# A transformer tower with a mixture of experts: the last tile four times in its rows, and expert weights halved in four pieces instead of eight

## Chip, cores, metric

The kernel runs on one core of one Trainium2 chip. The metric is the device time of one execution in microseconds (us). The engines are TensorE (PE), VectorE (DVE), ScalarE (ACT), GpSimd (POOL) and SyncE (SP), which issues most of the transfers.

## The reference

Float32 throughout. 32 images give 36 patches and a class token each: T = 1184 tokens of 256. Cut to what matters:

```python
h = concat([class_token, patches @ W.T + b]) + pos_embedding
# attention inside a token, over its 16 heads of 16 (not over tokens)
q, k, v = heads(ln(ln(h)) @ Wq, Wk, Wv);  q = elu(q) + 1;  k = elu(k) + 1
kv  = einsum('bhnd,bhne->bnde', k, v);  qkv = einsum('bhnd,bnde->bhne', q, kv)
attn = qkv / einsum('bhnd,bnd->bhn', q, k.sum(axis=1))[..., None]
x = ln(h) + attn @ Wo + bo
x = x + gelu(ln(x) @ Wfc + bfc) @ Wproj + bproj
h = h + x
# experts choose tokens: each of 16 takes its 148 best
y = ln(h);  scores = softmax(y @ gate.T).T;  w, idx = top_k(scores, 148)
eo = (gelu(y[idx] @ Wg.T) * (y[idx] @ Wu.T)) @ Wd.T * w
out = h + scatter_add(eo, idx) + (gelu(y @ Sg.T) * (y @ Su.T)) @ Sd.T
```

## The kernel before

**Order.** The code writes out one queue for each engine by hand, with semaphores between them; an instruction waits only for its semaphores and for what stands ahead in its own queue. There are three stages: ten tiles of 128 tokens through embedding, attention and MLP; the choice of each expert's tokens; sixteen experts one after the other.

**Tiles.** `turn(t)` on every engine works on several tiles at once: the attention of tile t, the output projection of t-1 and the MLP of t-2. 1184 = 9 x 128 + 32, so tile 9 (`s9`) has 32 real rows; the other 96 are computed too, and dropped. For a tile, PE makes q, k and v (`project_qk`, `project_v`), ACT makes exp(min(q,0)) (`negate_qk`, `exp_qk`), the DVE adds max(q,0) (`combine`). Then the DVE multiplies every head of q with every head of k, as two products of 128x2048 (`qk_product`), sums over the 16 elements of a head (`qk_sum`), divides by the row's sum (`normalise`) and multiplies with v (`v_product`, again two of 2048). PE adds up the products by transposing them on top of each other (`sum_values`, 2 x 16 matmuls), ACT copies (`turn_attn`), PE projects (`project_attn`), and `copy_x1`, `squares_c`, POOL's `norm_c` (reciprocal root), ACT's `norm_c`, `turn_x2`, PE's `mlp`, ACT's `gelu`, `project_mlp` and the DVE's `add_mlp` follow. `mlp` multiplies in float16: a float32 factor is halved into a float16 and a float16 rest, and three products are added. `rest_of_x2` on POOL makes one such rest. Then come `squares_f`, `norm_f`, `turn_y` and `logits`. `early(j)` puts the first four blocks of the shared expert between the tiles.

**Choice.** After the last `logits` the DVE makes the softmax (its first step is the maximum, line 1215) and looks for each expert's threshold in ten rounds, each with one small matmul; PE fills up with the shared expert (`fill(blocks)`, `fill(downs)`).

**Experts.** Two buffers `wex_s`, one being used, one being loaded. Gate and up weights (4096 columns of float32) are halved during the expert before: ACT writes the float16 half (`split_w`, count `whi_made`), the DVE the rest (`split_w`, line 1187, count `wlo_made`). The halves lie in the tile stage's weight buffers. PE works in four pairs of hidden blocks: `gate_up(s, p)`, then ACT's `gelu_e` and the DVE's `hidden` make the pair's activations, and `down(s, p)` multiplies them with the down weights. PE's order in an expert:

```python
gate_up(s, 0); down(s.off(-1), 3); gate_up(s, 1); turn_eo(s.off(-1)); slots(s)  # slots: experts 0 to 6
down(s, 0); gate_up(s, 2); turn_x(s.off(1)); down(s, 1); gate_up(s, 3); down(s, 2)
```

`gate_up(s, 0)` waits for half of the rests of the weights, `gate_up(s, 2)` for all. A pair p of `down` with p in `in_halves(s)` is multiplied in halves too: ACT makes `halve_down` and `halve_hidden`, the DVE `rest_of_down` and `rest_of_hidden`, and PE runs 12 float16 matmuls; otherwise it runs four float32 products of two instructions each. While slots for later experts are being found (experts 0 to 6, `s.finds`; DVE's `tokens`, `hot`), only pair 0 is halved; from expert 7 on pairs 0 and 1. `copy_eoT` on ACT takes the finished sums of the expert before, `weigh` scales them, POOL gathers rows and scatters results.

Of the kernel before, what the change touches and what calls it, by code (L numbers as in the profile page):

```python
# [21 lines left out]
P = 128  # L22
# [9 lines left out]
HH = H // 2  # L32
MLP = 1024
# [39 lines left out]
def in_halves(s):  # L73

    return (0,) if s.finds else (0, 1)
# [55 lines left out]
def vit_tower(nc, patches, sel, wtok, base, wqkv, bias, wo, wfc, wproj, cols, gate,  # L131
              wsh, wsd, wex, consts, out):
    with ExitStack() as ctx:
# [151 lines left out]
        base_part = [place1(D // 2)[0:3 * BASE].bitcast(BF16) for _ in range(2)]  # L285
        wfc_raw = wex_s[0][:, 0:nfc]
        wfc16 = [as16(wfc_s)[:, b * nfc:(b + 1) * nfc] for b in range(2)]

        def w16(par, part, piece):

            if par == 0:
                return as16((wfc_s, wproj_s)[part])[:, piece * n16:(piece + 1) * n16]
            if part == 0:
                return as16(wsh_s)[:, piece * n16:(piece + 1) * n16]
            if piece < 6:
                return as16(wtok_s)[:, piece * n16:(piece + 1) * n16]
# [33 lines left out]
        w_in = {n: sem(f"in_{n}") for n in ("bias", "consts", "tok", "qkv", "o", "proj", "moe")}  # L330
# [23 lines left out]
        prod_made, num_done = sem("prod_made"), sem("num_done")  # L354
# [35 lines left out]
        def halves_by(s, i):  # L390
# [3 lines left out]
            if s.finds:  # L394
                return s.times(1, i)
# [18 lines left out]
        CHAIN_ROUNDS = 74  # L414
# [5 lines left out]
        def _(sp):  # L420
# [51 lines left out]
            sp.dma_start(wsd_s[:], wsd).then_inc(w_in["moe"], 16)  # L472
            sp.wait_ge(fclo_made, 2)
# [40 lines left out]
        def _(gp):  # L514
# [70 lines left out]
            for t in range(TILES + 1):  # L585
# [46 lines left out]
            gp.wait_ge(num_done, 2 * TILES)  # L632
# [25 lines left out]
        def _(act):  # L658
# [106 lines left out]

            def turn_x2(s):
# [1187 lines left out]
```

## Time and profile before

| what | value |
|---|---|
| median of three runs (lowest, highest) | 445.29 us (444.38, 446.16) |
| the profiled execution, its own time | 444.82 us |
| its span, first to last instruction | 442.9 us |
| busy: PE, weight loads, DVE | 415.3, 370.6, 361.4 us |
| busy: ACT, POOL | 291.7, 210.8 us |
| mean granted clock of PE | 0.987 |

The busy times are of the span. A row of a timeline joins equal neighbours (x16); in brackets stands how long the engine had been idle and what it waited for. Matmuls overlap, so the next row's start, and not the row's end, tells what a group costs.

### The profile page before, as it was taken

The numbers are of one execution on the slowest core, as the hardware profiler recorded it, in microseconds if no ns is written. First come the engines' busy times: TensorE is split into PE (matmuls) and PEld (weight loads), VectorE is DVE, ScalarE is ACT, GpSimd is POOL, SyncE is SP. The second block draws the span as 40 slices with busy tenths as digits, with TensorE's granted clock in tenths as the row PEclk, the third lists the DMA queues.
The fourth block names the chain that finished last, engine by engine and source line by source line (L and its number), as shares of the span: only waits on it lengthen the run. The fifth ranks groups of instructions, "written<-read, shape, count | busy, mean of one in ns | idle before, by whom it ended". The sixth has DMA issues, their size and how long they took to land. (4 is left out here: it accounts for less than half of the span.)

```text
span 442.9 us, 11362 instructions
## 1 busy us (share of the span) xinstructions
PE 415.3 (94%) x4188; PEld 370.6 (84%) x4188; DVE 361.4 (82%) x613; ACT 291.7 (66%) x746; POOL 210.8 (48%) x238
## 2 busy tenths in 40 slices
PE   8799999999999998997999999999999999999980
PEld 4477878988888887886787699999999999999980
DVE  3899999899999999726998588888887888888830
ACT  3564586897788766377541066777777777788840
POOL 1337637777546112332350424555555676766222
PEclk9999999999999998999999999999999999999996
DMA  8811670000000000004402399988998999997411
GB/s 287 305 60 36 236 304 1 14 13 0 13 14 11 3 13 12 3 14 157 160 1 95 80 301 313 303 292 318 301 301 275 328 326 329 335 328 226 118 17 15
DMA packets 20481, 69.31 MB, mean 157 GB/s; under 512 B 4602, under 2 KB 11236, under 8 KB 14044
## 3 DMA queue, kind: packets, MB, share of 16 engines
q1 hardware_dynamic: 14252, 60.40, 38.0%
q0 software_dynamic: 4608, 5.41, 6.1%
q10 hardware_dynamic: 1584, 3.03, 1.8%
q8 instruction: 21, 0.34, 0.3%
q14 instruction: 16, 0.13, 0.1%
HBM read 63.50 MB, written 5.33 MB: 155 GB/s over the span
## 5 line engine op out<-in xcount | busy, mean ns | idle before, releaser
L611 POOL DMA_INDIRECT xg<-token_rows,slot_g x32 | 50.2, 1569 | 72.0 <-DVE slot_g L1338 46.5
L622 POOL DMA_INDIRECT out_rows<-scratch,slot_s x32 | 53.4, 1668 | 25.2 <-ACT scratch L958 16.7
L927 ACT ACTIVATE scratch<-bank 128x296 f32<-128x296 f32 x64 | 26.5, 414 | 42.9 <-PE bank L1803 42.9
L1803 PE MATMUL bank<-scratch,wfc_s 128*128 128x148 f16 x512 | 52.5, 227 | 1.1 <-DVE scratch L1237 1.1
L1803 PE MATMUL bank<-scratch,wsh_s 128*128 128x148 f16 x512 | 52.6, 227 | 0.0
L1803 PE MATMUL bank<-scratch,wproj_s 128*128 128x148 f16 x256 | 50.6, 227 | 0.0
L1828 PE MATMUL bank<-scratch,wex_s 128*128 128x148 f32 x312 | 47.5, 295 | 0.0
L1187 DVE SCALAR_TENSOR_TENSOR wproj_s<-wex_s,wfc_s 128x512 f16<-128x512 f32 x64 | 42.1, 686 | 5.6 <-ACT wfc_s L825 4.7
L1361 DVE SCALAR_TENSOR_TENSOR scratch<-bank,scratch 128x296 f32<-128x296 f32 x64 | 29.6, 462 | 20.4 <-ACT scratch L927 20.3
L1076 DVE TENSOR_TENSOR scratch<-qk 128x2048 f32<-128x2048 f32 x20 | 45.1, 2291 | 0.7 <-PE bank L1553 0.5
L1081 DVE TENSOR_REDUCE qkt<-scratch 128x128 f32<-128x2048 f32 x20 | 44.7, 2278 | 0.0
L1803 PEld LDWEIGHTS bank<-scratch,wfc_s 128*128 128x128 f16 x512 | 42.0, 98 | 1.7 <-issue 1.2
L1803 PEld LDWEIGHTS bank<-scratch,wsh_s 128*128 128x128 f16 x512 | 42.1, 98 | 0.5
L1828 PEld LDWEIGHTS bank<-scratch,wex_s 128*128 128x128 f32 x312 | 41.2, 190 | 0.2 <-DVE scratch L1361 0.2
L1803 PE MATMUL bank<-scratch,wtok_s 128*128 128x148 f16 x192 | 39.3, 227 | 0.0
L825 ACT ACTIVATE wsh_s<-wex_s 128x512 f16<-128x512 f32 x64 | 38.0, 630 | 0.0
L825 ACT ACTIVATE wfc_s<-wex_s 128x512 f16<-128x512 f32 x64 | 37.9, 629 | 0.0
L528 POOL TENSOR_TENSOR rstd<-tmp,nhalf 128x1 f32<-128x1 f32 x38 | 35.3, 928 | 3.2
L1539 PE MATMUL bank<-wproj_s,hidT 128*128 128x256 f32 x160 | 36.4, 380 | 0.0
L1526 PEld LDWEIGHTS bank<-x,wfc_s 128*128 128x128 f16 x480 | 29.2, 101 | 8.3 <-ACT x L770 4.4
L526 POOL TENSOR_SCALAR tmp<-spread 128x1 f32<-128x1 f32 x29 | 12.1, 417 | 47.8 <-issue 31.1
L1187 DVE SCALAR_TENSOR_TENSOR wtok_s<-wex_s,wsh_s 128x512 f16<-128x512 f32 x48 | 32.3, 686 | 2.8 <-ACT wsh_s L825 2.2
(216 smaller groups left out, 1037.2 us busy)
## 6 DMA issues: line engine op xcount, KB each, us to landing
wex_s<-in_wex SPq DMA_DIRECT2D x48, 1024.0 KB, 5.1
patch_s<-in_patches SPq DMA_DIRECT2D x6, 384.0 KB, 3.1
token_rows<-y_s SPq DMA_DIRECT2D x10, 128.0 KB, 1.7
out_rows<-h_all SPq DMA_DIRECT2D x5, 256.0 KB, 6.2
wex_s<-in_wfc ACTq DMA_DIRECT2D x2, 512.0 KB, 9.7
wproj_s<-in_wproj SPq DMA_DIRECT2D x1, 1024.0 KB, 7.9
wex_s<-in_wsh SPq DMA_DIRECT2D x1, 1024.0 KB, 6.6
wqkv_s<-in_wqkv ACTq DMA_DIRECT2D x1, 768.0 KB, 8.0
```

The costliest lines, as they stand in the source:

```text
L528: return gp.tensor_tensor(rstd[:, k:k + 1], tmp[:, k:k + 1], nhalf[:], ALU.pow)
L611: gp.indirect_dma_start(xg[s.par][:, k, :], None, rows, bass.IndirectOffsetOnAxis(slot_g[s.par][:, k:k + 1], 0))\
L622: gp.indirect_dma_start(out, bass.IndirectOffsetOnAxis(slot_s[s.par][:, k:k + 1], 0), eo[2 * s.par + k], None, compute_op=ALU.add).then_in ...
L825: act.activation(w16(s.par, 0, PIECES[n]), wex_s[s.par][:, n * n16:(n + 1) * n16], ACT.Copy, scale=SPLIT).then_inc(whi_made, 1)
L1076: ve.tensor_tensor(dst.rearrange("p (h j d) -> p h j d", h=HH, j=H), q, k, ALU.mult).then_inc(v_chain, 1)
L1081: ve.tensor_reduce(qkt[:, g * HH:(g + 1) * HH, :], src.rearrange("p (h j d) -> p h j d", h=HH, j=H), AX, ALU.add).then_inc(v_chain, 1)
L1187: ve.scalar_tensor_tensor(w16(s.par, 1, PIECES[n]), wex_s[s.par][:, n * n16:(n + 1) * n16], SPLIT, w16(s.par, 0, PIECES[n]), ALU.mult, ALU ...
L1361: ve.scalar_tensor_tensor(hexT[:, 2 * p:2 * p + 2, :].rearrange("p m c -> p (m c)"), ps_up[p % 2][:, 0:2 * C], (HSPLIT if p in in_halves(s ...
L1526: last = pe.matmul(ps_fc[m // 4][:, (m % 4) * P:(m % 4 + 1) * P], wfc16[a][:, k * MLP + m * P:k * MLP + (m + 1) * P], x2_16[b][:, k, :], s ...
L1539: last = pe.matmul(ps_proj[:, 0:D], hidT[:, m, :], wproj_s[:, m, :], start=False, stop=(m == MC - 1))
L1803: last = pe.matmul(dst[p % 2][:, x * C:(x + 1) * C], w16(s.par, a, piece)[:, lo:lo + P], x16[s.par][b][:, k, :], start=(n == 0), stop=(n = ...
L1828: last = pe.matmul(ps_down[k][:, 0:C], wex_s[s.par][:, lo:lo + P], hexT[:, m, :], start=(m == 0), stop=(m == MC - 1))
```

## The change

It has two parts.

**The last tile.** The host lays the 32 rows of tile 9 four times below each other. Attention of the group of heads 4r to 4r+3 is then computed in rows 32r to 32r+31 only: the DVE's products are 128x1024 instead of four times 128x2048. The transposes on PE are 8 instead of 32, and `project_attn_last` multiplies four groups of 32 columns with four blocks of the output weights (`wo9`, four new loads on SP's queue ahead of expert 0's weights) into the first 32 rows. The queues of PE, ACT, POOL and the DVE are written in a new order around tile 9.

**The experts.** Weights are halved in four pieces of 1024 columns, not eight of 512, in a new order among the other steps; and pairs 0 and 1 are halved in all sixteen experts. The places of the halves change so that two pieces lie side by side (`two_of`).

```diff
 def in_halves(s):
-    return (0,) if s.finds else (0, 1)
+    return (0, 1)
...
+            for x in range(2):
+                for b in range(2):
+                    sp.dma_start(wo9[b * HG * HD:(b + 1) * HG * HD, x::2, :], wo[x * HG * HD:(x + 1) * HG * HD, :, :]).then_inc(w_in["o9"], 16)
             sp.wait_ge(fclo_made, 2)
             load_gu(Step(0, 0), 0)
...
 # POOL, tile loop
+                if t == TILES:
+                    norm_c(s.off(-1), after(2))
                 if t >= 2:
                     rest_of_x2(s.off(-2))
...
-                if t >= 1:
+                if 1 <= t < TILES:
                     norm_c(s.off(-1), after(2))
...
 # ACT, split_w (the DVE's in the same way)
-                    act.activation(w16(s.par, 0, PIECES[n]), wex_s[s.par][:, n * n16:(n + 1) * n16],
-                                   ACT.Copy, scale=SPLIT).then_inc(whi_made, 1)
+                    act.activation(two_of(s.par, 0, n), wex_s[s.par][:, 2 * n * n16:2 * (n + 1) * n16],
+                                   ACT.Copy, scale=SPLIT).then_inc(whi_made, 2)
...
 # ACT, end of the tiles
-            for t in range(3, TILES):
+            for t in range(3, TILES - 1):
                 turn(t)
             s9 = Step(0, TILES - 1)
+            turn_attn(s9.off(-1))
+            norm_c(s9.off(-2))
+            squares_f(s9.off(-3))
+            copy_x1(s9.off(-1))
+            turn_x2(s9.off(-2))
+            squares_c(s9.off(-1))
+            load_gelu()
+            turn_attn_last()
             norm_c(s9.off(-1))
-            turn_x2(s9.off(-1))
-            squares_f(s9.off(-2))
-            turn_attn(s9)
+            gelu(s9.off(-2))
+            norm_f(s9.off(-3))
             copy_x1(s9)
             squares_c(s9)
-            gelu(s9.off(-1), (0,))
+            turn_x2(s9.off(-1))
+            turn_y(s9.off(-3))
+            squares_f(s9.off(-2))
             norm_c(s9)
-            gelu(s9.off(-1), (1,))
+            gelu(s9.off(-1))
             turn_x2(s9)
...
-            split_w(Step(0, 0), range(0, 3))
+            split_w(Step(0, 0), (0,))
             squares_f(s9)
...
-            split_w(Step(0, 0), range(3, 6))
+            split_w(Step(0, 0), (1, 2))
             turn_y(s9)
...
 # ACT, expert
                 halve_down(s, 0)
                 if not first:
                     copy_eoT(s.off(-1))
+                halve_hidden(s, 0)
                 split(0)
-                halve_hidden(s, 0)
-                split(1)
                 gelu_e(s, 1)
-                split(2)
                 halve_down(s, 1)
                 halve_hidden(s, 1)
-                split(3)
+                split(1)
                 if not first:
                     weigh(s.off(-1))
-                split(4)
                 gelu_e(s, 2)
                 if not last:
                     turn_x(s.off(1))
-                split(5, 6, 7)
+                split(2, 3)
                 gelu_e(s, 3)
...
 # DVE, last tile: combine_last(s), then turn_last(s)
+                for r in range(GROUPS):
+                    mine, own = slice(r * LAST, (r + 1) * LAST), slice(r * n, (r + 1) * n)
+                    ve.scalar_tensor_tensor(qk[s.par][mine, 0:n], ps_qk[mine, own], 0.0, expo[mine, own], ALU.max, ALU.add)\
+                      .then_inc(own_made, 1)
+                ve.wait_ge(own_made, GROUPS)
+                ve.scalar_tensor_tensor(qk[s.par][:, D:2 * D], ps_qk[:, D:2 * D], 0.0, expo[:, D:2 * D], ALU.max, ALU.add).then_inc(qk_made, 1)
...
+                add_mlp(s.off(-3))
+                # product 128x1024, sum over 16, sum over a head's row, reciprocal, weights, product 128x1024
...
 # DVE, end of the tiles
+            halve_shared()
+            cast_marks()
             add_mlp(s9.off(-2))
-            halve_shared()
             halve_y(0, 3)
-            cast_marks()
             add_mlp(s9.off(-1))
...
 # DVE, expert
+                rest_of_hidden(s, 0)
                 split(0)
-                rest_of_hidden(s, 0)
-                split(1)
                 hidden(s, 1)
                 if not first:
                     place(s.off(-1))
-                split(2)
                 rest_of_down(s, 1)
                 rest_of_hidden(s, 1)
...
-                split(3, 4)
+                split(1)
                 hidden(s, 2)
                 if nxt:
                     split_x(s.off(1))
-                split(5, 6, 7)
+                split(2, 3)
                 hidden(s, 3)
...
 # PE, end of the tiles
-            for t in range(4, TILES):
+            for t in range(4, TILES - 1):
                 turn(t)
-            early(0, 1)
             s9 = Step(0, TILES - 1)
+            sum_values(s9.off(-1))
+            project_attn(s9.off(-1))
+            turn_x2(s9.off(-2))
+            sum_values_last(s9)
+            mlp(s9.off(-2))
+            project_attn_last(s9)
             turn_x2(s9.off(-1))
-            sum_values(s9)
-            project_attn(s9)
+            logits(TILES - 5)
+            project_mlp(s9.off(-2))
+            pe.wait_ge(x1_made, TILES)
+            turn_y(s9.off(-3))
+            early(0)
             mlp(s9.off(-1))
-            logits(TILES - 4)
             turn_x2(s9)
             project_mlp(s9.off(-1))
             turn_y(s9.off(-2))
             mlp(s9)
+            early(1)
             project_mlp(s9)
             early(2)
+            pe.wait_ge(yT_made, TILES - 3)
+            logits(TILES - 4)
```

## Rows read from the trace of the kernel before

**Rows 1.** TensorE's timeline, last tile: start, us, engine, line, operation, idle before.

```profile
167.48 0.40 PE L1526 MATMUL bank<-x,wfc_s 128*128 128x128 f16 x4 [1.50 <-ACT x L770]
168.23 4.26 PE L1526 MATMUL bank<-x,wfc_s 128*128 128x128 f16 x44 [0.35 <-POOL x L562]
...
181.26 1.97 PE L1553 MATMUL bank<-kst,scratch 128*128 128x128 f32 x16 [0.90 <-ACT x2T L741]
...
186.42 2.84 PE L1526 MATMUL bank<-x,wfc_s 128*128 128x128 f16 x48
...
190.23 0.44 PE L1440 MATMUL bank<-kst,x 128*128 128x128 f32 x2 [0.56 <-ACT x L717]
...
197.08 3.68 PE L1539 MATMUL bank<-wproj_s,hidT 128*128 128x256 f32 x16
```

**Rows 2.** VectorE's timeline, last tile and the softmax's first step.

```profile
161.62 0.68 DVE L1106 SCALAR_TENSOR_TENSOR qk<-bank,expo 128x512 f32<-128x512 f32 x1
...
174.95 2.29 DVE L1095 TENSOR_TENSOR late<-qkt,vx 128x2048 f32<-128x2048 f32 x1
...
207.56 0.32 DVE L1215 TENSOR_REDUCE mx<-bank 128x10 f32<-128x160 f32 x1
```

**Rows 3.** ScalarE's timeline in experts with search and without.

```profile
277.58 0.48 ACT L933 ACTIVATE scratch<-bank 128x148 f32<-128x148 f32 x2
...
289.11 0.48 ACT L933 ACTIVATE scratch<-bank 128x148 f32<-128x148 f32 x2
...
345.91 0.48 ACT L933 ACTIVATE scratch<-bank 128x148 f32<-128x148 f32 x2
346.27 0.63 ACT L825 ACTIVATE wsh_s<-wex_s 128x512 f16<-128x512 f32 x1
346.79 0.45 ACT L949 ACTIVATE scratch<-scratch 128x296 f16<-128x296 f32 x1
...
350.01 0.82 ACT L958 ACTIVATE scratch<-bank,weight 74x256 f32<-74x256 f32 x2
...
351.84 1.67 ACT L825 ACTIVATE wsh_s<-wex_s 128x512 f16<-128x512 f32 x3
...
356.61 0.48 ACT L933 ACTIVATE scratch<-bank 128x148 f32<-128x148 f32 x2
```

**Rows 4.** VectorE's timeline in an expert without search.

```profile
351.49 0.69 DVE L1187 SCALAR_TENSOR_TENSOR wtok_s<-wex_s,wsh_s 128x512 f16<-128x512 f32 x1 [0.15 <-ACT wsh_s L825]
...
354.65 0.46 DVE L1361 SCALAR_TENSOR_TENSOR scratch<-bank,scratch 128x296 f32<-128x296 f32 x1
```

**Rows 5.** TensorE's timeline in experts with search and without.

```profile
271.12 1.22 PE L1828 MATMUL bank<-scratch,wex_s 128*128 128x148 f32 x8
272.18 0.29 PE L1803 MATMUL bank<-scratch,wsh_s 128*128 128x148 f16 x2
...
350.01 0.42 PE L1780 MATMUL bank<-kst,xg 74*128 74x74 f32 x4
350.42 0.95 PE L1821 MATMUL bank<-scratch,x_all 128*128 128x148 f16 x12
351.21 0.29 PE L1803 MATMUL bank<-scratch,wfc_s 128*128 128x148 f16 x2
...
355.35 0.84 PE L1828 MATMUL bank<-scratch,wex_s 128*128 128x148 f32 x5
```

**Rows 6.** One line's instructions: line 1059, duration in ns minimum/median/maximum.

```profile
L1059 DVE SCALAR_TENSOR_TENSOR wfc_s<-wex_s,wfc_s x2: 1224/1225/1226, 16.2 to 18.0; 128x1024 f16<-128x1024 f32 x2
```

**Rows 7.** Stretches: busy of five engines (x instructions), granted clock, DMA share, GB/s.

```profile
168.00:170.00 2.00, 1.77 (x17) 1.77 (x18) 2.00 (x2) 1.73 (x4) 1.75 (x5) 0.57 0.00 0
204.00:208.00 4.00, 2.70 (x26) 2.27 (x24) 2.56 (x6) 3.84 (x7) 0.88 (x2) 1.00 0.48 152
```

**Rows 8.** ScalarE's timeline at the end of the last tile.

```profile
204.14 0.60 ACT L717 ACTIVATE y_s<-h_all,shift,rstd 128x256 f32<-128x256 f32 x1 [1.03 <-POOL shift L533]
204.65 1.66 ACT L825 ACTIVATE wfc_s<-wex_s 128x512 f16<-128x512 f32 x3
```

More of the change, by code:

```diff
@@ L32 @@
 HH = H // 2
+GROUPS = 4
+HG = H // GROUPS
+LAST = 32
 MLP = 1024
@@ L285, in vit_tower @@
         base_part = [place1(D // 2)[0:3 * BASE].bitcast(BF16) for _ in range(2)]
+        wo9 = place1(GROUPS * D).rearrange("p (r n) -> p r n", r=GROUPS)
         wfc_raw = wex_s[0][:, 0:nfc]
@@ L1175, in turn, with turn_last @@
                 v_product(s, 1, late[:], scaled)
-                if t + 1 < TILES:
+                if t + 2 < TILES:
                     combine(s.off(1))
-            for t in range(TILES):
+                else:
+                    combine_last(s.off(1))
+            def turn_last(s):
+                by = [P, HG, H, HD]
+                mine = prod[s.par][:, 0:HG * H * HD]
+                weights = qkt[:, 0:HG, :]
+                add_mlp(s.off(-3))
+                ve.wait_ge(qk_made, TILES)
+                q = qk[s.par][:, 0:HG * HD].rearrange("p (h d) -> p h d", d=HD).unsqueeze(2).to_broadcast(by)
+                k = qk[s.par][:, D:2 * D].rearrange("p (j d) -> p j d", d=HD).unsqueeze(1).to_broadcast(by)
+                at = after(5)
+                ve.tensor_tensor(mine.rearrange("p (h j d) -> p h j d", h=HG, j=H), q, k, ALU.mult).then_inc(v_chain, 1)
+                ve.wait_ge(v_chain, at(1))
+                ve.tensor_reduce(weights, mine.rearrange("p (h j d) -> p h j d", h=HG, j=H), AX, ALU.add).then_inc(v_chain, 1)
+                ve.wait_ge(v_chain, at(2))
+                ve.tensor_reduce(den[:, 0:HG], weights, AX, ALU.add).then_inc(v_chain, 1)
+                ve.wait_ge(v_chain, at(3))
+                ve.reciprocal(rden[:, 0:HG], den[:, 0:HG]).then_inc(v_chain, 1)
+                ve.wait_ge(v_chain, at(4))
+                ve.tensor_tensor(weights, weights, rden[:, 0:HG].unsqueeze(2).to_broadcast([P, HG, H]), ALU.mult).then_inc(v_chain, 1)
+                ve.wait_ge(v_made, TILES)
+                ve.wait_ge(v_chain, at(5))
+                a = weights.rearrange("p h j -> p j h").unsqueeze(3).to_broadcast([P, H, HG, HD])
+                v = vx[s.par][:].unsqueeze(2).to_broadcast([P, H, HG, HD])
+                ve.tensor_tensor(mine.rearrange("p (j h e) -> p j h e", j=H, h=HG), a, v, ALU.mult).then_inc(prod_made, 1)
@@ L1199, in _ @@
             add_mlp(s9)
[L1200 removed]
+            split_w(Step(0, 0), (0,))
             shared_hidden(2)
[L1202 removed]
+            split_w(Step(0, 0), (1, 2))
             shared_hidden(3)
@@ L1555, in sum_values, with sum_values_last, project_attn_last @@
                     last.then_inc(num_done, 1)
+            def sum_values_last(s):
+                pe.wait_ge(x2T_made, TILES - 2)
+                pe.wait_ge(prod_made, s.times(2, 1))
+                for n in range(H // 2):
+                    last = pe.matmul(ps_at[:, 0:P], prod[s.par][:, n * P:(n + 1) * P], ident,
+                                     is_transpose=True, start=(n == 0), stop=(n == H // 2 - 1))
+                last.then_inc(num_done, 1)
+            def project_attn_last(s):
+                pe.wait_ge(x1_made, s.n)
+                pe.matmul(ps_o[:, 0:D], ident, x_all[:, s.n, :], start=True, stop=False)
+                pe.wait_ge(attnT_made, TILES)
+                pe.wait_ge(w_in["o9"], 64)
+                for r in range(GROUPS):
+                    pe.matmul(ps_o[0:LAST, 0:D], attnT[:, 0, r * LAST:(r + 1) * LAST], wo9[:, r, :], start=False, stop=False)
+                pe.matmul(ps_o[:, 0:D], ones_b[0:BP, :], bias_s[:, B_O:B_O + D], start=False, stop=True).then_inc(o_done, 1)
             def shared_gate_up(j):
@@ L1888, in _lay_out @@
     tok[:T].reshape(IMAGES, SEQ, PATCH_K)[:, 1:] = x
+    assert T == (TILES - 1) * P + LAST
+    tok[T:] = np.tile(tok[T - LAST:T], (GROUPS - 1, 1))
     a = {"patches": np.ascontiguousarray(tok.reshape(TILES, P, TKC, P).transpose(0, 3, 2, 1))}
@@ L1894, in _lay_out @@
     sel[np.where(t % SEQ == 0, SEQ + 1, SEQ), t] = 1
+    sel[:, T:] = np.tile(sel[:, T - LAST:T], (1, GROUPS - 1))
     in_halves = np.isin(np.arange(TP) // P, SPLIT_TILES)
```

49 lines of the change are left out of this document (29 added, 20 removed).

## The prediction

> **What bounds the kernel now.** I read the table of stretches first, then TensorE's timeline, then those of VectorE (DVE) and ScalarE (ACT) at the same moments. The page says PE 94% busy, DVE 82%, ACT 66%, and the chain that ended last holds only the last scatter, so neither tells what an edit is worth. Three stages matter. In the tile loop (to 160 us) PE and DVE are both full. In the last tile (160 to 207 us) they take turns: PE has nothing ready from 165.98 us, waits twice, for ACT and for POOL, and then runs slowly [rows 1]; the DVE works on the last tile's attention until 177.24 us [rows 2]. From 253 us on the sixteen experts run, PE without a gap: one expert with pair search takes 11.53 us (289.11 less 277.58), one without 10.70 us (356.61 less 345.91) [rows 3]. What the reader is to see there is how little room is behind the full PE: the last hidden pair of an expert is ready at 354.65 + 0.46 = 355.11 us, and PE starts the matmuls that need it at 355.35 us [rows 4, 5]. With about 0.08 us for the signal the slack is 0.16 us in a round of 10.70.
>
> **The last tile on the DVE.** From the halving instruction at 512 columns, 0.69 us [rows 4], and the same at 1024, 1.225 us [rows 6], one column costs 1.045 ns and an instruction 0.15 us; the products of 2048 columns fit (2.29) [rows 2]. Removed are four products and two sums of 2048 with their small ones. In their place: combine as four pieces of 32x64 (0.21 each) and one of 256 (0.42), with overlap 1.1 us instead of 0.6; add_mlp 0.35; product 1.22, sum 1.22, three small instructions 0.75 with waits, product 1.22. From 161.62 us the last product is ready at 167.6 instead of 177.24 us.
>
> **The last tile on PE.** PE is free at 165.98 in both. Before, it waits until 168.23 us and its 48 matmuls end at about 172.3. Now `sum_values_last` stands ahead of `mlp(7)` and waits for the DVE until 167.7; eight transposes take 0.9 us at full clock (16 take 1.97) [rows 1]. The granted clock after the old gap was 0.57 in 168 to 170 us, while 1.3 us without work in 204 to 208 us left it at 1.00 [rows 7]. The new gap of 1.7 us lies between. I take it that the clock falls as before to the lower of its two levels, which makes `mlp(7)` end at 172.6, 0.3 us later than before; if it does not, at 171.4.
>
> The Trainium skill ("TensorE: Matmul & The Clock Gate", Terms and Part 1) says that the clock has just these two states and that the activity window is free-running, so that the same gap may or may not cost a fall. By that rule the new gap could go either way from run to run, and the sum would be 1.1 us better with no fall; the trace agrees as far as a gap of 1.3 us did not cost it and 1.85 us did.
>
> From there to the end of `project_mlp(9)` (197.08 + 3.68 = 200.76 us before) PE loses: 32 transposes, 3.55; the waits of 0.90 and 0.56 us before 181.26 and 190.23 [rows 1], for both of which the new order has other work (`early(0)`, `project_mlp`); the logits moved behind, 0.57 (from 189.10, where the 48 matmuls of 186.42 stop issuing, to the wait's start at 189.67); tails that these waits exposed, 0.2. It gains two more products of 256 columns in `project_attn_last`, 0.43 each as in the 3.68 us for eight, 0.85. Sum 5.0 less. The end of `project_mlp(9)` comes at about 196.0, 4.7 us earlier. The reordered queues of ACT and POOL I followed step by step: `norm_c(8)` waits for POOL ahead of `gelu(7)` until about 171.2 and costs nothing, since `project_mlp(7)` now starts at 176; the rest of `x2T` of the last tile is ready near 187.0, `mlp(9)` wants it near 187.8: that cover is thin, and each us it is late is one us of PE. The four loads of `wo9` go on SP's queue at 50 us, 0.43 us each, before weights that are needed 150 us later: nothing.
>
> **Up to the search.** What follows `project_mlp(9)` is serial: add, squares, POOL's root, `norm_f(9)` on ACT 3.38 us later (204.14 before), then halvings, and the DVE's first step of the softmax at 207.56, 3.42 us after `norm_f(9)` [rows 2, 8]. Before, three halvings of 512 stand there (first one through ACT at 204.65 + 0.63, then 3 x 0.60 on the DVE, then 0.34 for the last shared product). Now two of 1024, a third more columns: ACT starts 0.51 after `norm_f(9)`, 1.05, 0.15 for the signal, 2 x 1.14 (1.225 less the overlap of 0.08), 0.34: 4.33. So 0.9 us is given back, and the search begins 3.9 us earlier (5.0 with no fall of the clock). The search itself, 45 us, keeps its instructions: its one piece of 1024 for two of 512 lies before a wait of the DVE for PE. Front: -3.9 us.
>
> **The experts: PE.** In experts 0 to 6 the second down pair turns from 8 float32 matmuls (1.06 us from start to next start) to 12 float16 (0.79, of which the others' show a wait of 0.16 us for the halved weights before them: 350.01 + 0.25 to 350.42) [rows 5]. Alone that is 7 x 0.27 = 1.9 us less, and the pieces' new order takes the 0.16 us away in eight more, 1.3 us.
>
> **The experts: the loop behind PE.** Larger pieces save overlap only: on ACT 0.63 for 512 against, by the slope of the rows of 512 and 296 columns (0.63, 0.45), 1.05 for 1024; started back to back 1.04 (two) against 0.94. DVE 1.21 against 1.14. That is 0.4 and 0.3 us per expert; but each piece now stands whole in a loop through three engines. From the end of the last hidden pair: signal to PE 0.08; down pair 1.06; to ACT 0.20 (355.35 + 1.06 to 356.61); `copy_eoT` 0.36; `halve_hidden` 0.34; first piece on ACT 1.05; to the DVE 0.15; first piece there 1.14; `hidden(1)` 0.46; 0.03; `halve_hidden(1)` 0.34; second piece on ACT 0.94; `weigh`, `gelu_e(2)` and `turn_x` 1.31 (350.01 to 351.84 less one piece of 0.52); third piece 1.05; to the DVE 0.15; third and fourth piece there 2.28; `hidden(3)` 0.46 [rows 3 to 6]. Sum 11.40 us. The same loop before is 10.5, since the DVE works on a piece of 512 while ACT makes the next and `hidden(1)` waits behind 0.6, not 1.14 us. PE's own round is 10.54, so the eight last experts go from 10.70 to 11.40 us: 8 x 0.70 = 5.6 us more, PE waiting 0.8 us for `hidden(3)` in each. Where the search for slots makes PE's own round 11.28, the loop decides by little: 11.40 against 11.53, 5 x 0.13 = 0.65 less. The first expert with its neighbour come out even. Experts: +4.9 us. Bounds: pieces on ACT of 1.00 to 1.11 and on the DVE of 1.20 to 1.25 make it +2.2 to +7.5. What DMA brings is not late: gate and up weights are asked for about a round and a half before use, and a longer round helps them.
>
> **Sum.** -3.9 + 4.9 = +1.0 us. The profiled execution took 444.82 us (442.9 of span, 1.9 around it), which becomes 445.8; the median of the runs shown is 0.47 above the profiled one, so 446.3 us. 0.5% (2.2 us) is what a measurement can tell from nothing: no change that can be told.
>
> **Rivals.**
> - The loop is hidden after all (PE's full rounds speak for it; the slack of 0.16 us against it): the experts take PE's own time, -1.9 - 1.3, with -3.9 in front 438.2 us. It needs pieces 0.12 us cheaper than estimated at all six places. Chance 0.12.
> - The loop is longer: pieces at the upper bound, 11.6 us, now above the old round even with search: +7.8, and -3 in front, 450 us. It decides once the loop passes 11.5. Chance 0.15.
> - The last tile's gain does not arrive: `mlp(9)` waits for ACT's and POOL's `x2T`, or `gelu(7)` behind `norm_c(8)` holds `project_mlp(7)`; worth 3 us if ACT is that late: -1 + 4.9, 449.2 us. For it speaks how much ACT has in order there; against it the slack of 0.8 us and more that I found. 0.10.
> - The clock stays up after the gap at 166 us: 445.2 us. 0.20.
> - PE waits so often in the experts that its clock falls in each: at the lower clock 44 of the 48 matmuls took 4.26 us, all 48 took 2.84 [rows 1], so about 1.1 us for each fall, 8 x 1.1 more, 455 us. The Trainium skill (the same page, "HAM oscillation — how this bites in real kernels") describes loops that fall each round, with longer waits; gaps here of 0.9 and 1.3 us left the clock at 1.00 [rows 1, 7]. 0.03.
>
> **How the numbers follow.** The forecast has 0.40, with its own range 444.5 to 448. Faster by over 0.5% (below 443.1): the hidden loop and a little of the fourth rival, 0.15. Slower (above 447.5): second, third and last rival, 0.28. Same: 0.57. The range 442 to 449.5 leaves out the hidden loop, the upper part of the longer one and the falling clock, 0.20.
>
> **What would show it.** In the new trace: the last product of the last tile ends near 167.6 us; the first reduction of the softmax near 203.7; `copy_eoT` comes every 11.4 us in all experts but the first, and PE waits 0.7 to 0.8 us for `hidden(3)` before each last down pair of experts 7 to 14. If PE shows no gap there, the loop's sum is wrong; if the search starts later than 205, the order in the last tile.

## The result, and the profile after

| | before | changed |
|---|---|---|
| median on record (lowest, highest; executions) | 445.1 us (444.38, 446.16; 4) | 449.93 us (448.04, 450.74; 4) |
| ratio, 95% interval | | 1.0104 (1.0077 to 1.0131) |
| profiled execution: own time, span | 444.82, 442.9 us | 448.04, 445.6 us |
| first `combine` on the DVE, from the span's start | 20.58 us | 21.16 us |
| from there to the softmax's first step | 186.98 us | 183.31 us |
| from there to the first `copy_eoT` | 58.50 us | 58.77 us |
| the fourteen rounds from one `copy_eoT` to the next | 6 x 11.525, 8 x 10.70 us | 14 x 11.455 us |
| from the first `combine` to the last `copy_eoT` | 409.13 us | 411.37 us |

The prediction was 446.3 us with "no change that can be told"; on record the kernel became 1.0% slower, and 449.93 lies 0.4 us above the range. The lower part of the table comes from the two traces and has no start and no end in it. There the change costs 2.24 us; the forecast sum was 1.0. The profiled execution of the changed kernel was the fastest of its four, 1.89 us below their median.

The profile page after, the parts on busy time and on the costliest groups (busy us, mean ns, idle us and what ended it):

```profile
PE 414.0 (93%) x4196; PEld 366.9 (82%) x4196; DVE 355.8 (80%) x564; ACT 290.3 (65%) x696; POOL 196.2 (44%) x238
...
L1252 DVE SCALAR_TENSOR_TENSOR wproj_s<-wex_s,wfc_s 128x1024 f16<-128x1024 f32 x32 | 38.5, 1224 | 11.6 <-ACT wfc_s L845 11.6
L1921 PE MATMUL bank<-scratch,wex_s 128*128 128x148 f32 x256 | 40.2, 301 | 4.7 <-DVE scratch L1426 4.7
```

Every engine has less to do than before, and the kernel is slower: PE now waits 4.7 us in all for `hidden` ahead of a down pair. TensorE's timeline in the last tile:

```profile
168.45 1.81 PE L1626 MATMUL bank<-kst,scratch 128*128 128x128 f32 x8 [2.03 <-DVE scratch L1241]
170.05 3.79 PE L1589 MATMUL bank<-x,wfc_s 128*128 128x128 f16 x48
173.67 0.65 PE L1633 MATMUL bank<-x_all,kst 128*128 128x256 f32 x2
...
193.59 3.62 PE L1602 MATMUL bank<-wproj_s,hidT 128*128 128x256 f32 x16
```

The waits of 0.90 and 0.56 us in [rows 1] are gone, and `project_mlp(9)` starts 172.43 us after the first `combine` (193.59 - 21.16) instead of 176.50 (197.08 - 20.58). The long idle time ahead of the last tile's sums is 2.03 us, and behind it the clock is low, as in the first row of [rows 7] (the granted clock is the first number behind the five pairs):

```profile
168.00:172.00 4.00, 3.55 (x27) 3.52 (x28) 3.97 (x3) 2.36 (x5) 3.92 (x3) 0.58 0.00 0
```

The end of that stretch, on ScalarE and on VectorE, against [rows 8] and the last of [rows 2]:

```profile
200.17 0.60 ACT L733 ACTIVATE y_s<-h_all,shift,rstd 128x256 f32<-128x256 f32 x1 [0.17 <-POOL shift L547]
200.68 1.99 ACT L845 ACTIVATE wfc_s<-wex_s 128x1024 f16<-128x1024 f32 x2
```

```profile
201.86 2.36 DVE L1252 SCALAR_TENSOR_TENSOR wproj_s<-wex_s,wfc_s 128x1024 f16<-128x1024 f32 x2 [2.42 <-ACT wfc_s L845]
204.14 0.42 DVE L1151 SCALAR_TENSOR_TENSOR hsh_s<-bank,gel_sh 128x256 f32<-128x256 f32 x1
204.47 0.31 DVE L1280 TENSOR_REDUCE mx<-bank 128x10 f32<-128x160 f32 x1
```

The DVE idles 2.42 us for two pieces on ACT and then works alone: two engines in turn. From `norm_f(9)` to the softmax it is 4.30 us (forecast 4.33).

One round of a late expert: ScalarE, VectorE and TensorE, the counterparts of [rows 3 to 5]:

```profile
354.89 0.48 ACT L962 ACTIVATE scratch<-bank 128x148 f32<-128x148 f32 x2 [0.92 <-PE bank L1921]
355.25 0.45 ACT L978 ACTIVATE scratch<-scratch 128x296 f16<-128x296 f32 x1
355.59 1.06 ACT L845 ACTIVATE wfc_s<-wex_s 128x1024 f16<-128x1024 f32 x1
...
358.43 0.45 ACT L978 ACTIVATE scratch<-scratch 128x296 f16<-128x296 f32 x1 [0.95 <-DVE scratch L1426]
358.79 1.04 ACT L845 ACTIVATE wfc_s<-wex_s 128x1024 f16<-128x1024 f32 x1
359.73 0.81 ACT L987 ACTIVATE scratch<-bank,weight 74x256 f32<-74x256 f32 x2
...
361.04 2.00 ACT L845 ACTIVATE wfc_s<-wex_s 128x1024 f16<-128x1024 f32 x2
...
366.34 0.48 ACT L962 ACTIVATE scratch<-bank 128x148 f32<-128x148 f32 x2 [0.92 <-PE bank L1921]
```

```profile
356.79 1.23 DVE L1252 SCALAR_TENSOR_TENSOR wproj_s<-wex_s,wfc_s 128x1024 f16<-128x1024 f32 x1 [0.59 <-ACT wfc_s L845]
357.94 0.46 DVE L1426 SCALAR_TENSOR_TENSOR scratch<-bank,scratch 128x296 f32<-128x296 f32 x1
...
362.24 2.36 DVE L1252 SCALAR_TENSOR_TENSOR wproj_s<-wex_s,wfc_s 128x1024 f16<-128x1024 f32 x2 [0.29 <-ACT wfc_s L845]
364.51 0.89 DVE L1426 SCALAR_TENSOR_TENSOR scratch<-bank,scratch 128x296 f32<-128x296 f32 x2
```

```profile
353.57 1.27 PE L1921 MATMUL bank<-scratch,wex_s 128*128 128x148 f32 x8 [0.58 <-DVE scratch L1426]
365.03 1.27 PE L1921 MATMUL bank<-scratch,wex_s 128*128 128x148 f32 x8 [0.58 <-DVE scratch L1426]
```

Read the loop by start times. PE 353.57, ACT's copy 354.89, `halve_hidden` 355.25, first piece 355.59, the DVE's 356.79, `hidden(1)` 357.94, `halve_hidden(1)` 358.43, second piece 358.79, `weigh` 359.73, third piece 361.04, the DVE's last two 362.24, `hidden(3)` 364.51, PE again 365.03. It closes in 11.46 us and nothing in it has slack. PE shows 0.58 us of emptiness (forecast 0.7 to 0.8), and the round costs 0.755 more than before.

### The profile page after: what moved, and what is told of

The parts are those of the page before. It is cut to its first block and busy times, and to the rows that moved or that the text cites. A ratio compares the mean times of both kernels' runs of the same rounds, so it can differ in the third digit from the quotient of the medians.

```text
span 445.6 us, 11224 instructions
## 1 busy us (share of the span) xinstructions
PE 414.0 (93%) x4196; PEld 366.9 (82%) x4196; DVE 355.8 (80%) x564; ACT 290.3 (65%) x696; POOL 196.2 (44%) x238
## 5 line engine op out<-in xcount | busy, mean ns | idle before, releaser
L627 POOL DMA_INDIRECT xg<-token_rows,slot_g x32 | 36.7, 1148 | 65.3 <-DVE slot_g L1403 39.1
L1252 DVE SCALAR_TENSOR_TENSOR wproj_s<-wex_s,wfc_s 128x1024 f16<-128x1024 f32 x32 | 38.5, 1224 | 11.6 <-ACT wfc_s L845 11.6
L1921 PE MATMUL bank<-scratch,wex_s 128*128 128x148 f32 x256 | 40.2, 301 | 4.7 <-DVE scratch L1426 4.7
L1102 DVE TENSOR_TENSOR scratch<-qk 128x2048 f32<-128x2048 f32 x18 | 40.6, 2290 | 0.5 <-PE bank L1616 0.4
L1921 PEld LDWEIGHTS bank<-scratch,wex_s 128*128 128x128 f32 x256 | 33.7, 190 | 8.1 <-DVE scratch L1426 7.4
L1107 DVE TENSOR_REDUCE qkt<-scratch 128x128 f32<-128x2048 f32 x18 | 40.2, 2276 | 0.0
L1602 PEld LDWEIGHTS bank<-wproj_s,hidT 128*128 128x128 f32 x160 | 29.6, 190 | 3.8
L845 ACT ACTIVATE wsh_s<-wex_s 128x1024 f16<-128x1024 f32 x32 | 32.8, 1052 | 0.0
L845 ACT ACTIVATE wfc_s<-wex_s 128x1024 f16<-128x1024 f32 x32 | 32.8, 1051 | 0.0
L1589 PE MATMUL bank<-x,wfc_s 128*128 128x128 f16 x480 | 30.6, 223 | 0.6
```

The costliest lines, as they stand in the source:

```text
L627: gp.indirect_dma_start(xg[s.par][:, k, :], None, rows, bass.IndirectOffsetOnAxis(slot_g[s.par][:, k:k + 1], 0))\
L845: act.activation(two_of(s.par, 0, n), wex_s[s.par][:, 2 * n * n16:2 * (n + 1) * n16], ACT.Copy, scale=SPLIT).then_inc(whi_made, 2)
L1102: ve.tensor_tensor(dst.rearrange("p (h j d) -> p h j d", h=HH, j=H), q, k, ALU.mult).then_inc(v_chain, 1)
L1107: ve.tensor_reduce(qkt[:, g * HH:(g + 1) * HH, :], src.rearrange("p (h j d) -> p h j d", h=HH, j=H), AX, ALU.add).then_inc(v_chain, 1)
L1252: ve.scalar_tensor_tensor(two_of(s.par, 1, n), wex_s[s.par][:, 2 * n * n16:2 * (n + 1) * n16], SPLIT, two_of(s.par, 0, n), ALU.mult, ALU.s ...
L1589: last = pe.matmul(ps_fc[m // 4][:, (m % 4) * P:(m % 4 + 1) * P], wfc16[a][:, k * MLP + m * P:k * MLP + (m + 1) * P], x2_16[b][:, k, :], s ...
```

## The experiments

One row for each, in the order they are told. Medians in us with lowest, highest and number of executions; "before" is the kernel before, run on the same chip beside it; the last three columns are times of the trace after the first `combine` (itself in the column ahead of them). Four chips: the first four rows belong to one, the next four to a second, the next two to a third and the last two to a fourth.

| edit | median | before | ratio (95%) | first `combine` | softmax | first to last `copy_eoT` | last `copy_eoT` |
|---|---|---|---|---|---|---|---|
| changed kernel again | 447.77 (446.64, 449.32; 7) | 445.37 | 1.0065 (1.0037 to 1.0093) | 20.16 | 183.27 | 169.25 | 411.27 |
| last tile only | 442.25 (439.65, 442.99; 8) | 445.37 | 0.9927 (0.9899 to 0.9956) | 20.65 | 182.79 | 163.63 | 404.89 |
| experts only | 451.82 (449.85, 453.82; 6) | 445.37 | 1.0150 (1.0112 to 1.0189) | 23.55 | 185.60 | 169.32 | 413.68 |
| last tile, two pairs, eight pieces | 441.87 (439.73, 443.79; 10) | 445.37 | 0.9928 (0.9903 to 0.9954) | 21.12 | 182.74 | 163.46 | 405.26 |
| `hidden(3)` ahead of the last piece | 442.27 (440.96, 445.13; 6) | 445.5 | 0.9929 (0.9901 to 0.9957) | 22.81 | 183.19 | 162.37 | 404.33 |
| gap filled | 448.82 (448.12, 448.89; 4) | 445.5 | 1.0067 (1.0046 to 1.0087) | 22.04 | 183.13 | 169.26 | 411.15 |
| large pieces, old pairs | 448.0 (447.2, 450.65; 6) | 445.5 | 1.0050 (1.0032 to 1.0068) | 23.31 | 182.98 | 169.69 | 412.27 |
| gap filled and `hidden(3)` ahead | 441.75 (440.02, 442.9; 6) | 445.5 | 0.9903 (0.9880 to 0.9927) | 22.63 | 183.12 | 162.25 | 404.14 |
| gap filled, halvings held back | 447.59 (445.13, 448.2; 12) | 446.64 | 1.0009 (0.9989 to 1.0030) | 20.57 | 181.67 | 169.35 | 409.79 |
| all three | 440.54 (439.79, 441.57; 6) | 446.64 | 0.9860 (0.9832 to 0.9888) | 22.29 | 181.70 | 162.60 | 403.07 |
| before again | 449.09 (447.2, 450.02; 12) | 448.31 | 1.0012 (0.9991 to 1.0032) | 21.33 | 186.92 | 166.99 | 412.38 |
| changed, a third time | 449.0 (448.07, 450.36; 12) | 448.31 | 1.0013 (0.9992 to 1.0033) | 22.16 | 183.20 | 169.31 | 411.84 |

(For the two traces above the column "first to last `copy_eoT`" is 163.65 before and 169.29 after. From the first `combine` to that of the last tile it is 140.75 to 141.05 us in all fourteen.)

### The changed kernel again

No edit.

> The changed kernel once more. Its trace is 2.7 us longer than that of before, while the medians stand 4.8 us apart. Theory (the loop through ScalarE and VectorE, 11.46 us in every expert, minus some 3 us in the last tile): median 448 to 450, rounds of 11.46 us again. Rival (the other 2 us are the clock, which falls once more in some executions, around the new gap of TensorE at 166 us): the traces differ by the stretches of lower clock, with a mean clock of 0.982 in the longer ones.

The trace repeats itself within 0.1 us (411.27), the time does not: 0.65% above before where the record has 1.04%, and its median, 447.77 us, is just below the 448 to 450 expected. The rival on the clock is taken up where the prediction is answered.

### The last tile's part alone

The changed kernel, with the pieces, their order and the pairs of before:

```diff
-    return (0, 1)
+    return (0,) if s.finds else (0, 1)
...
-                split(2, 3)
+                split(5, 6, 7)
                 gelu_e(s, 3)
```

> Only the last tile's part; the experts as before. Theory: rounds of 11.53 and 10.70 us again, the search begins 3 to 4 us earlier, 3 us faster than before, 442. Rival (the gap at 166 us costs clock, or the new order costs elsewhere): 444 to 446, no gain.

The last tile's part is worth 4.2 us of the trace (409.13 - 404.89), and the time is 0.73% less. 0.5 us of it comes with small pieces: the softmax is at 182.79, with large ones at 183.31.

### The experts' part alone

The kernel before, with the other half of the change:

```diff
-    return (0,) if s.finds else (0, 1)
+    return (0, 1)
...
-                split(5, 6, 7)
+                split(2, 3)
                 gelu_e(s, 3)
```

> Only the experts' part (pieces of 1024, two halved pairs everywhere); the last tile as before. Theory: rounds of 11.46 us in all experts, 5.6 us slower than before plus some 0.3 from the early pieces, 451. Rival (TensorE's own work decides, pieces do not matter): 1.9 to 3 us faster, 442.

Rounds of 11.46 us: +5.7 us from first to last `copy_eoT` (169.32 against 163.65), the time 1.5% more. The softmax comes 1.4 us earlier than before with the old last tile, since here the clock stayed up behind the same gap that [rows 1] show. TensorE's timeline:

```profile
170.23 0.40 PE L1526 MATMUL bank<-x,wfc_s 128*128 128x128 f16 x4 [1.50 <-ACT x L775]
170.98 2.63 PE L1526 MATMUL bank<-x,wfc_s 128*128 128x128 f16 x44 [0.35 <-POOL x L567]
```

Before, the same 44 matmuls behind the same two waits took 4.26 us.

### The last tile with two pairs everywhere, eight small pieces

```diff
 # the last tile's part alone, and
-    return (0,) if s.finds else (0, 1)
+    return (0, 1)
```

> The last tile's part and two halved pairs everywhere, but eight pieces of 512 in the old order. Theory (the size of the pieces is the cause): rounds of about 11.4 us with search and 10.70 without, -3 in the last tile and -0.3 to -0.7 in the experts, 441.5. Rival (two halved pairs in the experts with search load ScalarE and VectorE too much): those rounds at 11.6 or more, 443 to 446.

The pairs are worth nothing that can be told: 163.46 us for the rounds against 163.63, and 0.6 us lost between the softmax and the first `copy_eoT` (59.06 us against 58.47); 0.9928 against 0.9927. The whole loss is in the pieces and their order.

### hidden(3) ahead of the last piece

```diff
 # ACT, and on the DVE hidden(s, 3) for gelu_e
-                split(2, 3)
-                gelu_e(s, 3)
+                split(2)
+                gelu_e(s, 3)
+                split(3)
```

> The changed kernel with the last of the four pieces behind gelu_e(3) on ScalarE and behind hidden(3) on VectorE; all sizes as changed. Theory: this takes 1.14 us (VectorE's piece) out of the loop of 11.46, to about 10.3, below TensorE's own work, so rounds of 11.28 with search and 10.6 without; 6 x 0.25 and 8 x 0.10 below before, with the last tile 5 to 6 us faster than before, 440. Rival (the two engines are simply slower with large pieces, or another wait of the same length takes over): rounds of 11 us or more without search, 445 or more.

Same pieces, same instructions, one of them two places later. VectorE's timeline:

```profile
351.97 0.46 DVE L1427 SCALAR_TENSOR_TENSOR scratch<-bank,scratch 128x296 f32<-128x296 f32 x1
352.35 1.22 DVE L1253 SCALAR_TENSOR_TENSOR wqkv_s<-wex_s,wsh_s 128x1024 f16<-128x1024 f32 x1
353.52 0.47 DVE L1427 SCALAR_TENSOR_TENSOR scratch<-bank,scratch 128x296 f32<-128x296 f32 x1
354.58 0.69 DVE L1450 SCALAR_TENSOR_TENSOR x_all<-wex_s,x_all 128x512 f16<-128x512 f32 x1 [0.60 <-ACT x_all L971]
```

`hidden(3)` stands behind one piece (352.35 to 353.52), and PE no longer waits for it at all: rounds of 10.65 us (one 10.87), below the old 10.70, and of 11.29 to 11.43 with search. 6.9 us less than the changed kernel in the rounds. The sizes are the same, so the loss came from where the last piece stands in the loop, not from large pieces as such. The time, 442.27 us, is 3.2 us below before on its chip and not the 5 to 6 expected: the loop was put at 10.3 us and the rounds at 11.28 and 10.6, and they are a little longer.

### The gap filled

```diff
             turn_x2(s9.off(-2))
+            for _ in range(26):
+                pe.matmul(bank[0][:, 384:512], ones_b[:], ones_b[:], start=True, stop=True)
             sum_values_last(s9)
```

Work is added here whose result nobody uses.

> The changed kernel with 26 matmuls of 128x128 float16-sized data into an unused part of a bank in the gap ahead of sum_values_last (some 1.6 of its 2.0 us). Theory: the clock then stays at its upper level and the transposes and mlp(7) take 0.9 and 2.8 us, 1.1 to 1.9 us less than in the changed kernel, 446.5. Rival (the clock falls for another reason, or the end of mlp(7) is not what the rest waits for): the search begins at the same distance from the first combine, 183.3 us.

The clock is 1.00 over 168 to 172 us, the eight transposes start every 0.11 us (0.90 in all, against 1.60) and `mlp(7)` takes 2.84. From the start of the transposes to the end of `mlp(7)` that is 3.58 us instead of 5.22 (173.67 - 168.45), 1.64 less. The softmax comes only 0.2 us earlier. What took the rest: TensorE's, then GpSimd's timeline.

```profile
169.28 1.06 PE L1627 MATMUL bank<-kst,scratch 128*128 128x128 f32 x8 [0.58 <-DVE scratch L1242]
170.18 2.84 PE L1590 MATMUL bank<-x,wfc_s 128*128 128x128 f16 x48
...
176.49 0.44 PE L1504 MATMUL bank<-kst,x 128*128 128x128 f32 x2 [0.92 <-ACT x L734]
```

```profile
169.63 1.70 POOL L582 TENSOR_TENSOR hx<-h_all,x_all 128x256 f32<-128x256 f32 x1
171.42 2.12 POOL L541 TENSOR_SCALAR tmp<-spread 128x1 f32<-128x1 f32 x1
```

PE reaches `turn_x2(8)` earlier and waits 0.92 us for ACT's `norm_c(8)`, which waits for GpSimd, whose smallest instruction takes 2.12 us there.

### Large pieces, old pairs

```diff
-    return (0, 1)
+    return (0,) if s.finds else (0, 1)
```

> The changed kernel with pair 1 of down plain again in the experts with search; pieces of 1024. Theory: TensorE's own work is the bound there, 11.53 us, and the loop of 11.46 elsewhere: 6 x 0.07 us slower than the changed kernel, 448.3. Rival (the second halved pair loads the engines): faster than the changed kernel by 1 us or more.

Rounds with search 11.525, without 11.455: PE's own round decides in the first, the loop in the second. Here the clock stayed at 1.00 behind an unfilled gap of 2.04 us, and again PE waited 0.91 us for `norm_c(8)`.

### Gap filled and hidden(3) ahead

The two diffs above in one kernel.

> f_hidden_first and g_gap_filled together. Theory: the gains add, 438.5 to 439. Rival: as f_hidden_first, since the filled gap gives nothing.

The gains did not add (438.5 to 439 us was expected): both edits together give what the second gives alone, within 0.2 us of the trace.

### The halvings held back

```diff
 # with the gap filled; DVE
-            halve_shared()
             cast_marks()
+            ve.wait_ge(c_rstd, TILES - 1)
+            halve_shared()
             add_mlp(s9.off(-2))
```

> The changed kernel with the gap before the last tile's sums filled by 26 matmuls, and with VectorE's two halvings of 2048 columns held back until GpSimd has finished norm_c(8). Theory (GpSimd's small instructions are slowed by VectorE's long halvings, 2.12 us for a 128x1 tensor_scalar, 1.70 for hx, and this holds back norm_c(8), gelu(7) and project_mlp(7), which is where the clock's gain went in the run with the gap filled): GpSimd's rows read 0.73 and 0.19 us again, ScalarE's norm_c(8) comes about 3.5 us sooner, PE's wait of 0.92 us before turn_x2 is gone, and the search begins 182.0 us after the first combine, against 183.13 with the gap filled alone; time about 1.1 us below that run's. Rival (GpSimd is late for another reason, or project_mlp(7) is held by something else): 183.1, no change. Second rival (the halvings now hold back early(0) or the next halvings): search no earlier, or later.

GpSimd's timeline, then VectorE's and TensorE's:

```profile
168.21 0.72 POOL L582 TENSOR_TENSOR hx<-h_all,x_all 128x256 f32<-128x256 f32 x1
169.02 0.19 POOL L541 TENSOR_SCALAR tmp<-spread 128x1 f32<-128x1 f32 x1
169.29 0.55 POOL L543 TENSOR_TENSOR rstd<-tmp,nhalf 128x1 f32<-128x1 f32 x1
```

```profile
171.32 1.23 DVE L1157 TENSOR_SCALAR wsh_s<-wex_s 128x2048 f16<-128x2048 f32 x1 [2.17 <-POOL shift L548]
172.59 2.29 DVE L1159 SCALAR_TENSOR_TENSOR wsh_s<-wex_s,wsh_s 128x2048 f16<-128x2048 f32 x1
```

```profile
173.99 0.38 PE L1505 MATMUL bank<-kst,x 128*128 128x128 f32 x2
174.22 0.52 PE L1671 MATMUL bank<-gate_s,yT 128*128 128x16 f32 x4
```

The instruction of 2.12 us takes 0.19, PE has no wait ahead of `turn_x2(8)`, and the softmax comes at 181.67 us, 1.46 us earlier than with the gap filled alone (1.1 expected).

### All three

This wait, the filled gap and `hidden(3)` ahead of the last piece.

> The same with the last two pieces of weights parted, hidden(3) between them (both edits that helped or might help, together). Theory: search 182.0 to 182.3 us after the first combine, experts as in the run with hidden(3) ahead of the last piece (rounds of 11.3 to 11.4 and 10.65), the last copy_eoT 403.1 us after the first combine against 404.14 with the gap filled and hidden(3) ahead; time 440.7 us. Rival (the halvings' place doesn't matter): 404.1 and 441.8 us.

403.07 us to the last `copy_eoT`, as expected (403.1), 6.1 us below before; the time is 440.54 us, 1.4% below it. This version beats both kernels.

### Before again, and the changed kernel a third time

> The kernel before, unchanged, for a second trace of it and more executions. Theory (the first 20 us vary from execution to execution whatever the change, and what the change adds is the 2.2 us between the first combine and the last copy_eoT that the traces show): the last copy_eoT comes 409.1 us after the first combine again, within 0.1 us, while the first combine itself may come anywhere from 20.2 to 23.6 us. Rival (the kernel before starts reliably early, and the changed one late, so that part of the recorded difference of 4.8 us lies in the start): first combine at 20.6 us again.

> The changed kernel, unchanged, a third time. Theory: the last copy_eoT 411.3 us after the first combine, and a time 2.2 to 2.7 us (0.5% to 0.6%) above the kernel before on the same chip. Rival (the recorded 1.0% is the change's own): 4.5 us above it.

Of the two theories only the varying start held, and neither rival did: the last `copy_eoT` came at 412.38 us for 409.1 expected and at 411.84 for 411.3. On this chip the two kernels are level: 449.09 and 449.0 us. Ten of the twelve executions of the changed kernel are within 0.9 us of its median, and its trace reads 411.84. The kernel before is slower here (448.31 and 449.09 us) than on the other chips (445.1 to 446.64), and its trace shows 3.3 us in the experts with search, rounds of 13.60, 12.06, 11.53, 11.70, 11.69 and 11.92 us. TensorE's timeline in the first, and the stretches around it:

```profile
272.04 0.29 PE L1803 MATMUL bank<-scratch,wsh_s 128*128 128x148 f16 x2 [0.34 <-issue]
...
272.82 0.40 PE L1780 MATMUL bank<-kst,xg 74*128 74x74 f32 x3 [0.43 <-issue]
273.57 0.27 PE L1780 MATMUL bank<-kst,xg 74*128 74x74 f32 x1 [0.35 <-issue]
```

```profile
270.00:271.00 1.00, 1.00 (x19) 1.00 (x17) 0.58 (x1) 1.00 (x3) 0.56 (x1) 1.00 0.96 406
271.00:272.00 1.00, 0.66 (x8) 0.37 (x6) 0.44 (x3) 0.15 (x1) 0.84 (x1) 1.00 0.61 175
272.00:273.00 1.00, 0.53 (x6) 0.34 (x5) 1.00 (x2) 0.00 (x0) 0.70 (x2) 1.00 0.05 16
273.00:274.00 1.00, 0.65 (x7) 0.52 (x7) 0.18 (x1) 0.00 (x0) 1.00 (x1) 1.00 1.30 166
```

PE stops between matmuls that wait for no engine ("issue"), and ACT runs nothing from 272 to 274 us (fourth pair of columns): no semaphore that the trace shows explains it. The third trace of the changed kernel has one such stop, of 1.27 us, ahead of its first `copy_eoT`, and so has that of the large pieces with the old pairs. What makes them, and whether they favour one kernel, stays open.

The start, too, varied: 21.33 us here against 20.58 for the same kernel, though PE began tile 0's q and k earlier. TensorE's timeline here, then in the first trace of the kernel before:

```profile
16.75 3.25 PE L1492 MATMUL bank<-wqkv_s,xnT 128*128 128x512 f32 x4
```

```profile
17.36 1.88 PE L1492 MATMUL bank<-wqkv_s,xnT 128*128 128x512 f32 x4
```

The granted clock over 16 to 20 us is 0.57 here and 1.00 there. In all fourteen traces PE has waited 1.9 to 2.9 us for tile 0 just before. Behind that wait the clock fell in ten (0.57 to 0.84 over 16 to 20 us, of both kernels) and stayed at 1.00 in four; the two traces on record are among the four.

## Why the prediction was wrong

Two steps failed: the sum, in its sizes, and the way from the sum to the median.

**The sum.** "-3.9 + 4.9 = +1.0 us" is, in the two traces, -3.67, then +0.27 from the softmax to the first `copy_eoT`, then +5.64 in the rounds: +2.24. Both terms were right in sign and mechanism, and each part was mis-sized by 0.2 to 0.7 us, all to the same side. The largest is the experts' term, +5.64 for +4.9.

**The loop** was forecast at 11.40 us and measures 11.455, since from PE's start to ACT's copy it is 1.32 us and not 1.26; the other steps agree within 0.02. That is 8 x 0.055 = 0.44 us. In the rounds with search the loop is 0.07 below the old round, not 0.13, and there are six, not five: -0.42 for -0.65. That one length would stand in the rounds with and without search was right. That it is this loop is shown: with `hidden(3)` ahead of the last piece the eight rounds fall to 10.65.

**The pairs** were costed at 1.9 us less "alone". Alone they gave 0.2 us (163.63 to 163.46); why not more was not followed. In the changed kernel the loop covers them. PE's own round was put at 10.54 us; with the last piece moved, and no wait of PE left, it is 10.65.

**The last tile** was right in mechanism. "4.7 us earlier" at the end of `project_mlp(9)` was 4.07 (172.43 - 176.50). Most of the difference is at `mlp(7)`, which ended at 173.09 us on the clock of before (173.67 - 0.58) and not at 172.6: its fall of the clock costs 1.64 us and not the 1.2 between 172.6 and 171.4, and the eight transposes were costed "at full clock", 0.9 us, in the very case in which the clock was assumed to fall (1.60 by the rows). Most of it came back: from the start of `project_mlp(9)` to `norm_f(9)` it is 6.58 us (200.17 - 193.59) against 7.06 [rows 1, 8]. Of that 0.40 is one 128x1 instruction of GpSimd's root, 0.59 us before, beside a halving on the DVE, and 0.19 after. With 4.30 - 3.42 = 0.88 given back up to the softmax the search began 3.67 us earlier, not 3.9. Another 0.27 us goes between the softmax and the first `copy_eoT`, which the forecast had at nothing. It belongs to the experts' part (58.76 us with that part alone, 58.47 with the last tile alone, 58.50 before); where in it, was not tried.

**"Waits for POOL ahead of `gelu(7)` until about 171.2 and costs nothing"** was wrong in the time and right in the price. ACT's `norm_c(8)` came at 174.90:

```profile
174.90 0.60 ACT L733 ACTIVATE x<-x_all,shift,rstd 128x256 f32<-128x256 f32 x1 [4.33 <-POOL shift L547]
```

In the trace with the low clock PE arrives no sooner. But it takes away the fourth rival: with the clock up (gap filled, or by itself in the run with the old pairs) the gain was 0.2 to 0.3 us, not 1.1. The forecast had followed GpSimd's queue with the durations of before, when the DVE was running its sums of 2048 columns beside it; the change put `halve_shared` beside `norm_c(8)`, and that move was never costed. Holding it back returned the time.

**The rivals.** The hidden loop and the clock falling in every expert are refuted by the rounds. The longer loop (11.6, 450 us) and the last tile's gain not arriving (449.2 us) name about the time on record, but neither happened: 11.455, and -3.67.

**From the sum to the median.** The step was "444.82 us (442.9 of span, 1.9 around it), which becomes 445.8; the median of the runs shown is 0.47 above the profiled one, so 446.3 us": it took the start, the time around the span and the distance of the median to stay as they were. They did not. Of the 3.22 us between the two profiled executions 2.24 are above; the start is +0.58, what follows the last `copy_eoT` -0.12, and 0.52 lies outside the span (2.44 us around it, 1.92 before). And the changed kernel's median is 1.89 us above its profiled execution. So the miss of 3.6 us (449.93 for 446.3) is 1.2 for the sum, 0.5 for start and end, 0.5 around the span, and 1.4 for the median. The range had no term for the last three: the mis-sized terms alone make 447.5, inside the range and at the bound to "slower".

The 0.5 us around the span is the change's own, and is shown. In the 84 executions of the kernel before whose span was taken it is 1.89 to 2.00 us, and so it is in the 24 of the three variants that lack the large pieces or, in the experts with search, the second pair. Where both are in, it is 2.19 to 2.55 in 54 of 63 executions and 1.91 to 1.97 in nine. Why stays open.

The 1.4 us of the median is in part argued. The four executions on record have spans of 445.6, 446.9, 448.1 and 448.4 us at mean granted clocks of 0.988, 0.986, 0.982 and 0.982: the profiled one has the highest clock. The falls of the clock at the start, in ten of fourteen traces and in neither of the two on record, are one place where executions part: the rows of tile 0's q and k cost 1.37 us more with it (16.75 to 19.84 against 17.36 to 19.08). That the other three executions had this fall is not shown, since they left no trace, and on the last chip the changed kernel's spans do not follow the clock. The rival that put the rest on the gap at 166 us is not borne out: the clock is low there in the profiled execution, too.

The difference of the medians was 4.8 us on record, 2.4 in the second comparison and about 0 to 0.7 in the last. I take 2.2 us inside the span and 0.5 around it to be the change's own; that the rest is variation between executions and chips is argued from these numbers and not shown. That two rivals named a time near 449.93 is luck.

## What to carry to other kernels

- When a piece of work is made larger, don't add up overheads: write down the loop that passes through it, from engine to engine and back to where it began, and compare its length with the round of the full engine. Here fewer, larger instructions cost 5.6 us, and one instruction moved behind the one that the full engine waits for gave back 6.9.
- A reorder on one engine changes durations on its neighbour. Look up which instructions will now run side by side, and take the duration from rows where they did.
- If the wanted effect is 0.5%, read it between two marks inside the trace and measure it on more than one chip. Don't hang the median on one profiled execution: here that was the fastest of four.

## What the runs showed of the hardware

**GpSimd beside VectorE.** In the changed kernel's trace a 128x1 instruction on GpSimd took 2.11 us (0.19 elsewhere), an addition of 256 columns 1.70 (0.72), while the DVE's halvings took 1.70 and 2.69 us (1.23 and 2.29 with GpSimd kept away). GpSimd's timeline, then VectorE's:

```profile
168.80 1.70 POOL L581 TENSOR_TENSOR hx<-h_all,x_all 128x256 f32<-128x256 f32 x1
170.58 2.11 POOL L540 TENSOR_SCALAR tmp<-spread 128x1 f32<-128x1 f32 x1
```

```profile
168.22 1.70 DVE L1156 TENSOR_SCALAR wsh_s<-wex_s 128x2048 f16<-128x2048 f32 x1
169.95 2.69 DVE L1158 SCALAR_TENSOR_TENSOR wsh_s<-wex_s,wsh_s 128x2048 f16<-128x2048 f32 x1
```

The one-column instruction ends at 172.69 us, the halving at 172.64. The Trainium skill ("SBUF — State Buffer", "SBUF: two separate sides") says that the two engines share a port pair which one of them holds for a whole instruction, a VectorE instruction in a two-port mode or with two SBUF inputs included, while the other is blocked. The trace agrees for the second halving, which has two inputs, in the end times and in that each engine lost time to the other, and before, beside the DVE's sums, which have one input, GpSimd was not slowed. The first halving has one input and cost GpSimd's addition time as well (1.70 for 0.72); whether it runs in a two-port mode no trace shows.

**The clock behind one and the same gap.** TensorE was empty for 2.03 or 2.04 us ahead of the sums in seven traces. In six the granted clock then went to its lower level (0.50 in slices of 1 us), in one it stayed at 1.00. Where it fell, it fell at different moments: with the eight transposes taking 1.81, 1.72 or 1.62 us in three traces, and only behind them (1.06 to 1.12 us) in the other three, whose `mlp(7)` took 4.45 to 4.47 us instead of 3.79 to 3.97. The price is the same each time: 5.21 to 5.23 us from the first transpose to the end of `mlp(7)`, and 3.58 with no fall. A mean over a fixed stretch hides that: over 168 to 172 us it reads 0.58, 0.60, 0.60, 0.57, 0.81, 0.88 and 1.00. Behind the old gap it reads 0.57, 0.71 and 1.00 in three traces. 26 small matmuls in the gap left about 0.6 us of emptiness and 1.00 in four of four. The Trainium skill ("TensorE: Matmul & The Clock Gate", Part 1) calls the activity window free-running; the traces agree, in that one and the same gap is followed by a fall sooner, later or not at all.
